# A graph layer, a linear attention and a quantised feed-forward block in one kernel: the second bias added by accumulating transfers, the counts taken up at later tiles, one piece of keys per group

## What is computed

```
xn = layernorm(x)
agg(h)[d] = sum over edges (s, d) of h[s];  mean = agg / max(deg, 1)
h   = relu(xn @ Ws0 + mean(xn) @ Wn0 + b0)
gnn = h @ Ws1 + mean(h) @ Wn1 + b1
Q, K = elu(xn @ Wq + bq) + 1, elu(xn @ Wk + bk) + 1;  V = xn @ Wv + bv
mix = gelu((Q * sum(K * V) / (Q * sum(K) + 1e-6)) @ Wo + bo)
x   = x + gnn + mix
out = x + ffn(layernorm(x))      # 16-bit activations, 4-bit block weights
```

## Time and profile before

| | us |
|---|---|
| median of three runs | 1212.84 (1212.08 to 1213.51) |
| profiled execution, its own time | 1213.64 |
| profiled execution, its span | 1211.8 |
| TensorE busy | 1157.4 (96%) |
| VectorE busy | 679.4 (56%) |
| GpSimd busy | 393.2 (32%) |
| ScalarE busy | 356.5 (29%) |
| mean granted TensorE clock | 0.986 of full speed |

### The profile page before, as it was taken

The page is one execution under the profiler, slowest core; times in us unless marked ns, Lnnn a source line. Parts: engine busy times, 40 slices in busy tenths (PEclk is TensorE's granted clock), DMA queues, the critical chain, the costliest instruction groups (busy, mean ns, idle before and its releaser), DMA issues.

```text
span 1211.8 us, 15245 instructions
## 1 busy us (share of the span) xinstructions
PE 1157.4 (96%) x6309; PEld 622.7 (51%) x6309; DVE 679.4 (56%) x1232; ACT 356.5 (29%) x446; POOL 393.2 (32%) x224
## 2 busy tenths in 40 slices
PE   4898999999999999995999999999999999999978
PEld 3554555555555554442444555444444445569934
DVE  7766947658475563335633444656564345582763
ACT  5634333333324323310521112222210012251640
POOL 1266767758677684677400000000000000000000
PEclk8999999999999999998999999999999999999989
DMA  9935344353442439532731034432220080000005
GB/s 259 339 81 140 65 100 99 71 135 50 103 85 37 98 71 311 128 53 58 271 109 39 22 116 162 127 105 88 87 87 35 18 156 1 1 1 1 2 8 161
DMA packets 156151, 117.61 MB, mean 97 GB/s; under 512 B 93401, under 2 KB 132569, under 8 KB 155058
## 3 DMA queue, kind: packets, MB, share of 16 engines
q1 hardware_dynamic: 86744, 103.41, 27.4%
q0 software_dynamic: 69024, 13.07, 8.4%
q10 hardware_dynamic: 314, 0.16, 0.0%
HBM read 90.13 MB, written 21.41 MB: 92 GB/s over the span
## 4 chain that ended last, share of the span: by engine, by line
PE 50%; DMA 21%; issue 14%; POOL 12%; DVE 2%; ACT 1%; SPq 0%; POOLq 0%; ACTq 0%; DVEq 0%
PE ps L1053 25%; DMA at_scratch<-copies,cell 18%; POOL at_scratch L598 12%; PE ps L1085 7%; PE ps L1114 6%; PE ps L1151 6%; PE ps L1181 3%; DMA at_scratch<-zeros 2%; DMA raw<-in_L_mix_Wk_dram 1%; PE ps L1123 1%; PE ps L1101 1%; PE ps L991 0%; DMA parts<-at_scratch 0%; POOL at_scratch L588 0%; DMA key_scratch<-key_r 0%
## 5 line engine op out<-in xcount | busy, mean ns | idle before, releaser
L598 POOL DMA_INDIRECT at_scratch<-copies,cell x160 | 345.6, 2160 | 173.6 <-DMA at_scratch<-copies,cell 93.7
L983 PE MATMUL ps<-xnT,whl 128*128 128x512 f16 (+1 forms) x2160 | 383.3, 340 | 0.0
L983 PEld LDWEIGHTS ps<-xnT,whl 128*128 128x128 f16 x2160 | 211.1, 98 | 169.9 <-issue 1.7
L1053 PE MATMUL ps<-hb,hT 128*128 128x512 f16 x960 | 207.7, 379 | 1.3 <-DVE hT L1516 1.3
L1053 PEld LDWEIGHTS ps<-hb,hT 128*128 128x128 f16 x960 | 93.9, 98 | 114.5 <-DVE hT L1516 1.8
L1053 PE MATMUL ps<-hb,xnT 128*128 128x512 f16 x480 | 105.9, 383 | 12.4 <-DVE hb L1386 12.4
L579 POOL PARTITION_ALL_REDUCE ag_fw<-am_fw x9 | 3.2, 354 | 317.0 <-DVE am_fw L1399 317.0
L1053 PE MATMUL ps<-hb,VT 128*128 128x512 f16 x480 | 103.9, 379 | 1.5 <-ACT S_b L740 1.5
L1085 PE MATMUL ps<-AT,P 125*128 125x512 f16 (+1 forms) x480 | 84.7, 339 | 0.0
L1053 PEld LDWEIGHTS ps<-hb,xnT 128*128 128x128 f16 x480 | 47.3, 99 | 69.9 <-DVE hb L1386 12.9
L1114 PE MATMUL ps<-P,AT 125*128 125x512 f16 x360 | 79.0, 379 | 0.0
(11 more groups left out here) (231 smaller groups left out, 1190.1 us busy)
## 6 DMA issues: line engine op xcount, KB each, us to landing
raw<-in_L_gnn_W_neigh_dram SPq DMA_DIRECT2D x32, 512.0 KB, 5.0
raw<-in_L_gnn_W_self_dram SPq DMA_DIRECT2D x24, 512.0 KB, 5.2
key_b<-key_scratch SPq DMA_DIRECT2D x8, 1250.0 KB, 8.8
raw<-in_L_mix_Wo_dram SPq DMA_DIRECT2D x16, 512.0 KB, 3.9
parts<-at_scratch POOLq DMA_DIRECT2D x20, 312.5 KB, 3.8
at_scratch<-zeros POOLq DMA_DIRECT2D x6, 1020.0 KB, 17.7
x_all<-in_x_dram SPq DMA_DIRECT2D x9, 512.0 KB
x_acc<-in_x_dram SPq DMA_DIRECT2D x9, 512.0 KB
```

The lines of the kernel that those rows point to most:

```text
L598: pool.indirect_dma_start(out=at_scr[c % 2][:, :], out_offset=bass.IndirectOffsetOnAxis(ap=cell[:, c:c + 1], axis=0), in_=copies[:, c:c + ...
L983: mm = pe.matmul(acc_of(c)[:, a:b], whl[:, i, wp, k, :], xnT[:, k, ap, a:b], start=(k == 0 and wp == 0 and ap == 0), stop=(k == KC - 1 and ...
L1053: mm = pe.matmul(half_bank(i), stationary[:, k, ap, t * TP:t * TP + P], hb[:, n % 2, k, wp, :], start=(k == 0 and wp == 0 and ap == 0), st ...
```

## The change

Four things change. The bias b1 is added to `x_acc` by transfers that accumulate, issued by GpSimd, in place of GpSimd's own additions, and `b1_ok` counts 16 for each. `PIECE_AT` gives group 0 one piece of keys in place of two and every later one up to group 6 one, and a group's piece is done after `chunk_lo(g + 1, 3)` in place of before it. The ten `counts` are taken up behind tiles 21, 22, 24, 25, 27, 28, 30, 31, 33 and 34 in place of 15, 17, 19, 21, 23, 25, 27, 29, 30 and 31. `DEG_TILE` goes from 33 to 36.

```diff
-    PIECE_AT = [(1, 2)] + [(g + 2,) if g + 2 < NPC else () for g in range(1, KC)]
+    PIECE_AT = [(g + 1,) if g + 1 < NPC else () for g in range(KC)]
...
-        DEG_TILE = 33
+        DEG_TILE = 36
...
-        PART_TILE = {i: s for s, i in enumerate((15, 17, 19, 21, 23, 25, 27, 29, 30, 31))}
+        PART_TILE = {i: s for s, i in enumerate((21, 22, 24, 25, 27, 28, 30, 31, 33, 34))}
...
                 elif s == 6:
-                    pool.wait_ge(b1_ok, NT)
+                    pool.wait_ge(b1_ok, 16 * NT)
...
                 pool.wait_ge(mm_free, NT + t + 1)
-                pool.tensor_tensor(x_acc[:TP, t, :], x_acc[:TP, t, :], b1_b[:TP, :], ALU.add).then_inc(b1_ok, 1)
+                pool.dma_start(x_acc[:TP, t, :], b1_b[:TP, :], accum_op=ALU.add).then_inc(b1_ok, 16)
...
                 v_low(g)
+                if g + 1 < KC:
+                    chunk_lo(g + 1, 3)
                 for p in PIECE_AT[g]:
                     cells(p)
-                if g + 1 < KC:
-                    chunk_lo(g + 1, 3)
-                else:
+                if g + 1 == KC:
...
                 if i == DEG_TILE:
-                    dve.wait_ge(b1_ok, NT)
+                    dve.wait_ge(b1_ok, 16 * NT)
                     degrees(0, 1024, 1)
```

## The result

| | before | changed |
|---|---|---|
| median of four runs, us | 1212.59 (1212.08 to 1213.51) | 1199.15 (1198.52 to 1200.12) |
| profiled execution, its own time | 1213.64 | 1198.72 |
| its span | 1211.8 | 1196.9 |
| mean granted clock | 0.986 | 0.993 |

The ratio of the changed kernel to the one before is 0.9889, with a 95% interval of 0.9872 to 0.9906: 13.4 us less by the medians, 14.9 between the two profiled executions.

A forecast was written before the change was run, and what follows sets the result against it. TensorE, busy 96% of the span, was taken as the bound, with waits at group 1 and tile 20. Terms -7.8 - 14.1 + 6.3 = -15.6 from 1212.84 gave 1197.2 us, range 1190.5 to 1203.5.

The forecast's parts named there:

- the main case: The forecast of 1197.2 us with small offsets, 1195.5 to 1199.5; chance 0.70.
- Group 1, -7.8: TensorE's wait for ScalarE's squares in group 1 goes, with its slower clock: 7.8 us less.
- Tile 20, -14.1: TensorE's wait at tile 20 for weights held up behind the first count goes: 14.1 us less.
- The reciprocal, +6.3: New TensorE wait of 4.6 us after tile 39 for VectorE's reciprocal, plus 1.7 for the lower clock.
- Bias by transfer, 0: Ten accumulating transfers replace GpSimd's additions at 2.9 us each; VectorE is a few us late, costing TensorE nothing.
- The cover: Behind the tile where VectorE stands, TensorE takes five more tiles, 25.9 us, before it needs that tile's bank.
- its mark of 5.7 us a transfer: Slow bias transfers: from 5.7 us each, one by one, band 3 is late enough to stop TensorE.
- Whose scatter keeps its own pace: At tile 20: the scatter isn't moved by TensorE's earlier arrival, so the first band lands as before, 558.75.
- The sum: -7.8 - 14.1 + 6.3 = -15.6 us, taken from the median of 1212.84: 1197.2 us.
- No wait at the reciprocal: Rival: something unseen hides the new wait before the transposes, giving 1190.9 us; chance 0.08.
- The wait of group 1 stays: Rival: group 1's load is held by something else, giving 1205.0 us; chance 0.04.
- Slow transfers: Rival: slow bias transfers make bands late; chance 0.12 for part (1199.5 to 1210), 0.05 for no gain or loss.

The follow-up runs named there:

- the split kernel: The changed kernel with the reciprocal cut in two, 1024 columns behind tile 36 and 226 behind tile 38: 1192.14 us, ratio 0.9823.
- The filled wait: The changed kernel with twenty matmuls of unused result between tile 39 and the wait for the reciprocal: 1196.45 us, ratio 0.9891.
- the three kernels without a wait there: The changed kernel with the reciprocal cut in two (1192.14 us), that with GpSimd's bias additions (1191.44), and one with degrees and counts a tile earlier (1191.62).
- the transfers one by one: The changed kernel with GpSimd waiting for each bias transfer to land before going on: 1211.96 us, ratio 0.9998.

## Why the prediction was right

The time came out at 1199.15 where 1197.2 stood, inside the range and inside the main case.

- **Group 1, -7.8: measured -7.76.** From the first sum of squares to the third it took 44.13 + 52.70 us before; now it is 38.19 + 50.88 (74.95 to 113.14 to 164.02). The loads went out at 96.35 and 97.40, 1 us earlier than worked out, and the last square began at 106.26, a little later. The profile can't say which of the two edits did it; the runs with one of them show that either does. Kept as time it is only with the wait of tile 20 gone.
- **Tile 20, -14.1: measured -14.12.** Late counts alone do it. What the prediction left unsaid is that they also free the group's 7.8 us: with early counts and GpSimd's additions TensorE resumes 19.34 to 19.36 us after the bands in four executions out of four, so the two terms are a sum only because both edits were made. By the same tie the 14.1 holds for a scatter that ends as it did in that execution, at 554.62; another end gives another wait. On this chip the four runs before lay within 1.5 us, so one execution stood for them.
- **The reciprocal, +6.3: measured +7.4.** This is the term that was mis-sized. The wait is 4.60 as worked out: from 658.40, where tile 39 makes way (two tiles take 10.45 in the split kernel, 659.50 - 649.05, and they begin at 647.95), to 663.00. And the aggregation takes 86.35 from its start to the next product against 84.54: 1.8. What was left out is the ten transposes, which took 665.19 - 663.00 = 2.19 at the lower clock against 1.18. "One column each" was noted, but they weren't priced, and the term ends above the 6.4 that was its upper end. The filled wait and the three kernels without a wait there bear out both parts.
- **Bias by transfer, 0: right, with a price that was too low.** I took 2.9 us a transfer between 1.45 and 9.1; it was 5.0 in a row among other loads, and 7.5 with one in flight at a time. (The estimate from the Trainium skill's pages, Collectives: The Full Stack and SBUF — State Buffer, in the sections that the prediction names, was 2.4. The first of them tells of the halved pace for ReduceScatter, a collective. The measurement decides.) Two counts waited 2.94 and 2.21 us for their bands. In the execution seen the scatter had ended early, but that wasn't needed: in the split kernel the bands went out at 552.06, counts waited up to 7.34 us, and the time was still 1192.41. The cover was sized too small as well: TensorE stops six tiles, 31.2 us, behind the tile after which VectorE stands, and not five and 25.9. With that and the rest of the rival's sum as it stands, its mark of 5.7 us a transfer would be about 6.4, (606.7 + 5.2 - 561) / 8, an estimate.
- **"Whose scatter keeps its own pace"** doesn't hold as a fixed time. In twelve executions, one for each kernel, the bands went out between 533.84 and 554.62. The changed kernel's time didn't suffer, as the late counts hide it, but the kernel before has it in its time: it spread over 14.3 us on one chip, without its slowest run, where the prediction took 0.2% (2.4 us) as what can be told from no change. That the first chip was calm was luck.
- **The sum.** -7.76 - 14.12 + 7.42, and 0.45 by which the first sum of squares stood earlier (75.40 against 74.95), make -14.9, what the two profiled executions differ by. The forecast is 2.0 low by the median: 1.1 is the term above, 0.45 goes the other way by the earlier first sum, which wasn't forecast, and the rest is where each profiled execution lies to its median (0.80 above the 1212.84 from which the forecast started, 0.43 below now).
- **The rivals.** No wait at the reciprocal: no, the order is fixed. The wait of group 1 stays: no. Slow transfers: the mechanism is real, as the transfers one by one show. It didn't come true because several are in flight at once, which keeps them at 5.0, under its mark.

## What to carry to other kernels

When one engine waits for an event whose time is set elsewhere, a gain ahead of that wait is worth nothing until the wait is gone: measure the distance from the event to the restart, and if it stays fixed, move the consumer first. Price a new wait with all that follows it until the clock is back, small matmuls included, and then look for the one tile more of distance that makes it vanish. A wait that several edits could remove needs only one of them, so take the edits apart before keeping them all.

## What the runs showed of the hardware

- An accumulating transfer of 500 KB within SBUF lands in 7.5 us when it is the only one of its kind in flight, and ten take 5.0 each when several are; GpSimd spends 0.9 us to issue one (5.37 us for six).
- The granted clock fell 2.6, 5.3 and 3.6 us after the last matmul in the waits of 5.78, 12.41 and 4.53 us. With the transfers one by one it fell 3.1 us into the wait of 4.75, and stayed at full speed through the one of 3.37.
- A VectorE operation with both inputs in SBUF is stretched beside GpSimd's additions, 0.80 to 10.40 and 1.28 to 5.22, and stays at 0.81 beside the bias transfers.
- The scatter of 160 accumulating transfers ended at moments up to 20.8 us apart in twelve executions of twelve kernels; its own code is the same in all, but not when its pieces are worked out nor what runs beside it.
